# ScalarE copies the turned keys, squares the gated output and applies the first layer norm in place of VectorE

## What is computed

```python
q = rotate(silu(x @ Wq)); k = rotate(silu(x @ Wk)); v = x @ Wv      # per head
def step(S, qkv):                                                   # one chunk of 128 tokens
    scores = einsum('bthd,bshd->bhts', qi, ki) * D[None]            # D: causal mask with decay
    o_intra = einsum('bhts,bshd->bthd', scores, vi)
    o_inter = einsum('bthd,bhde->bthe', qi * decay_q, S)
    S_new = lam_C * S + einsum('bshd,bshe->bhde', ki * decay_k, vi)
    return S_new, o_intra + o_inter
g = o * sigmoid(x @ Wg1 @ Wg2)
g = g * rsqrt(mean(g * g, per head) + 1e-6) * norm_weight
x = layernorm(x + g @ Wo)
```

## Time and profile before

| | |
|---|---|
| time, three runs | 254.32, 258.5 and 258.65 us, median 258.5 |
| profiled execution, first to last instruction | 256.0 us |
| own time of the profiled execution | not listed; the three runs lie 1.7 below to 2.65 above its span |
| TensorE matmuls busy | 209.2 us (82%) |
| VectorE busy | 176.7 us (69%) |
| GpSimd busy | 114.0 us (45%) |
| ScalarE busy | 81.7 us (32%) |
| mean granted TensorE clock | 0.925 of full |

### The profile page before, as it was taken

One profiled execution on the slowest core, in us unless ns is written; L12 is line 12 of the kernel. 1 busy time (PEld: TensorE's weight loads), 2 busy tenths in 40 slices (PEclk: granted clock), 3 DMA queues, 4 the chain that ended last, 5 costly groups with the idle time before them and its releaser, 6 DMA issues.

```text
span 256.0 us, 3809 instructions
## 1 busy us (share of the span) xinstructions
PE 209.2 (82%) x1254; PEld 146.0 (57%) x1254; DVE 176.7 (69%) x438; ACT 81.7 (32%) x219; POOL 114.0 (45%) x188
## 2 busy tenths in 40 slices
PE   3788999995987798849799989999999997842461
PEld 1367555562745364515799776686786966411340
DVE  1168848779597979793556863348769788897751
ACT  0075664452432534241100113403223234423021
POOL 9661207335161413140516352346558529656352
PEclk9999999999799999977979999999999999995555
DMA  7990000000000000000000000000000001001011
GB/s 195 339 299 5 3 0 4 0 1 0 3 1 0 3 1 0 3 0 0 3 0 3 1 0 0 3 1 0 0 3 0 0 4 40 3 0 41 0 38 45
DMA packets 7027, 6.65 MB, mean 26 GB/s; under 512 B 1232, under 2 KB 6624, under 8 KB 7008
## 3 DMA queue, kind: packets, MB, share of 16 engines
q1 hardware_dynamic: 5744, 5.33, 6.6%
q10 hardware_dynamic: 1264, 1.08, 1.4%
HBM read 5.36 MB, written 1.05 MB: 25 GB/s over the span
## 4 chain that ended last, share of the span: by engine, by line
PE 52%; DVE 24%; issue 9%; POOL 6%; ACT 4%; DMA 3%; ACTq 1%; DVEq 0%; POOLq 0%
PE bank L1029 19%; PE bank L1230 12%; PE bank L1087 9%; PE bank L1244 4%; PE bank L1024 3%; DMA w_qk<-in_L_attn_Wk 3%; DVE hTe L776 2%; DVE w_qk L937 2%; PE bank L1132 2%; DVE stats L749 1%; POOL rstd L301 1%; DVE newton L685 1%; DVE probs L717 1%; PE bank L1120 1%; DVE newton L684 1%
## 5 line engine op out<-in xcount | busy, mean ns | idle before, releaser
L1087 PE MATMUL bank<-qx,kT 128*128 128x512 f32 x64 | 33.7, 652 | 10.6 <-DVE probs L717 8.9
L1230 PE MATMUL bank<-hTe,ctxT 128*128 128x128 f32 x256 | 31.7, 285 | 2.6 <-issue 2.6
L1230 PEld LDWEIGHTS bank<-hTe,ctxT 128*128 128x128 f32 x256 | 31.0, 201 | 3.2 <-issue 3.1
L499 ACT ACTIVATE qx<-bank,con 32x256 f32<-32x256 f32 x64 | 26.4, 458 | 16.0 <-PE bank L1024 15.4
L1244 PE MATMUL bank<-ctxT,aTe 128*128 128x256 f32 x128 | 29.0, 379 | 0.0
L284 POOL TENSOR_TENSOR rsin<-qk,rope_tab 128x256 f32<-128x256 f32 x16 | 13.2, 845 | 34.9 <-ACT qk L482 34.9
L1029 PE MATMUL bank<-f_w,oT 128*128 128x512 f32 (+4 forms) x80 | 28.0, 496 | 0.8 <-ACT oT L552 0.7
L298 POOL TENSOR_SCALAR rstd<-agg 128x1 f32<-128x1 f32 x24 | 5.3, 222 | 49.3 <-DVE agg L751 48.5
L1087 PEld LDWEIGHTS bank<-qx,kT 128*128 128x128 f32 x64 | 11.7, 197 | 26.8 <-issue 24.5
L717 DVE TENSOR_TENSOR probs<-bank,con 128x512 f32<-128x512 f32 x32 | 21.6, 686 | 5.8 <-PE bank L1087 5.0
L1244 PEld LDWEIGHTS bank<-ctxT,aTe 128*128 128x128 f32 x128 | 23.7, 190 | 2.9
(11 more groups left out here) (128 smaller groups left out, 407.7 us busy)
## 6 DMA issues: line engine op xcount, KB each, us to landing
x_sb<-in_x SPq DMA_DIRECT2D x4, 256.0 KB, 6.8
ctx_sb<-in_ctx SPq DMA_DIRECT2D x1, 1024.0 KB, 12.3
out<-x_sb SPq DMA_DIRECT2D x8, 128.0 KB, 1.7
fgo<-in_itok_BxS ACTq DMA_DIRECT2D x1, 512.0 KB, 9.3
con<-shape_constants SPq DMA_DIRECT2D x1, 338.5 KB, 3.0
w_v<-in_L_attn_Wv SPq DMA_DIRECT2D x1, 256.0 KB, 5.5
w_qk<-in_L_attn_Wq ACTq DMA_DIRECT2D x1, 256.0 KB, 5.7
w_qk<-in_L_attn_Wk ACTq DMA_DIRECT2D x1, 256.0 KB, 7.3
```

Source lines behind the costliest of these rows:

```text
L499: eng.activation(qx[rr, i % 2, :, 2 * r + par, :], two(bank[2][rr, 0:2 * P]), ACT.Copy, scale=con[rr, C_PARITY + par:C_PARITY + par + 1]). ...
L1087: eng.matmul(bank[3 + g % 2][:, :], kT[:, i % 2, g // 2, :], qx[:, i % 2, g // 2, 4 * (g % 2):4 * (g % 2) + 4, :].rearrange("p h n -> p (h ...
L1230: last = eng.matmul(bank[0][:, f * P:(f + 1) * P], ctxT[:, k, e, f * P:(f + 1) * P], hTe[:, j % 2, e, k, :], start=(e == 0 and k == 0), st ...
```

## The change

Three kinds of VectorE instructions go to ScalarE: the copy of the turned keys, the square of the gated output, and the application of the first layer norm. The last one has another form there (input times rstd plus a shift), so GpSimd computes that shift, minus mean times rstd, in one more instruction for each tile. Each engine's list is rewritten for it. On ScalarE the square stands ahead of the spreading of the queries and the key copy behind it. On VectorE the rest of `norm_o` moves behind `decay_state` (and, in round 7, behind the expert mask).

```diff
+            def ln0_scale(i):
+                ln_rstd(0, i)
+                eng.wait_ge(S_("ln0_rstd"), 2 * i + 2)
+                eng.tensor_scalar(shift[:, 0, i:i + 1], agg[:, 0, i, 0:1], rstd[:, 0, i:i + 1], -1.0,
+                                  ALU.mult, ALU.mult).then_inc(S_("ln0_shift"), 1)
...
-                        ln_rstd(0, i - 2)
+                        ln0_scale(i - 2)
...
+            def copy_kT(i):
+                eng.wait_ge(S_("kT_made"), i + 1)
+                if i >= 2:
+                    eng.wait_ge(S_("scores_made"), 4 * (i - 1))
+                eng.activation(kT[:, i % 2, :, :], two(bank[7][:, 0:D]), ACT.Copy).then_inc(S_("kT_copied"), 1)
+
+            def square_o(i):
+                eng.wait_ge(S_("gated"), i + 1)
+                if i >= 2:
+                    eng.wait_ge(S_("o_ms"), i - 1)
+                eng.activation(osq[:, i % 2, :], og[:, i % 2, :], ACT.Square).then_inc(S_("o_squared"), 1)
+
+            def apply_ln0(i):
+                eng.wait_ge(S_("ln0_shift"), i + 1)
+                eng.activation(h1[:, i, :], x1[:, i % 2, :], ACT.Identity, bias=shift[:, 0, i:i + 1],
+                               scale=rstd[:, 0, i:i + 1]).then_inc(S_("h1_done"), 1)
...
             def attention_round(i):
+                if i >= TILES:
+                    apply_ln0(i - 3)
+                if 0 <= i - 2 < TILES:
+                    square_o(i - 2)
                 if i < TILES:
                     expand_q(i)
+                    copy_kT(i)
                 if i + 1 < TILES:
                     silu_qk(i + 1)
+                if 0 <= i - 3 and i < TILES:
+                    apply_ln0(i - 3)
                 if i + 1 < TILES:
                     copy_v(i + 1)
...
             def attention_round(i):
-                if i < TILES:
-                    copy_kT(i)
...
-                if i >= TILES:
-                    ln_apply(0, i - 3, h1[:, i - 3, :], x1[:, (i - 3) % 2, :], "h1_done")
                 if 0 <= i - 2 < TILES:
                     gate_o(i - 2)
+                if i >= TILES and i - 2 < TILES:
                     norm_o(i - 2)
...
                 if i < TILES and i % 2 == 0:
                     decay_state(i // 2)
-                if 0 <= i - 3 and i < TILES:
-                    ln_apply(0, i - 3, h1[:, i - 3, :], x1[:, (i - 3) % 2, :], "h1_done")
+                if 0 <= i - 2 and i < TILES:
+                    norm_o(i - 2)
```

More of the change, by code:

```diff
@@ L151, in decoder_block @@
         rstd = sb("rstd", [P, 3, TILES])
-        shift = sb("shift", [P, TILES])
+        shift = sb("shift", [P, 2, TILES])
         newton = sb("newton", [P, 3, L * H])
@@ L425, in root_of_last @@
                             eng.wait_ge(S_("ln2_rstd"), 2 * n + 2)
-                            eng.tensor_scalar(shift[:, n:n + 1], agg[:, 2, n, 0:1], rstd[:, 2, n:n + 1], -1.0,
+                            eng.tensor_scalar(shift[:, 1, n:n + 1], agg[:, 2, n, 0:1], rstd[:, 2, n:n + 1], -1.0,
                                               ALU.mult, ALU.mult).then_inc(S_("shift"), 1)
@@ L464, in _ @@
                 if TILES <= r < TILES + 2:
-                    ln_rstd(0, r - 2)
+                    ln0_scale(r - 2)
         @block.scalar
@@ L582, in finish @@
                 eng.wait_ge(S_("shift"), j + 1)
-                eng.activation(y[:, ORDER[j], :], x3[:, j % 4, :], ACT.Identity, bias=shift[:, j:j + 1],
+                eng.activation(y[:, ORDER[j], :], x3[:, j % 4, :], ACT.Identity, bias=shift[:, 1, j:j + 1],
                                scale=rstd[:, 2, j:j + 1]).then_inc(S_("out_done"), 1)
@@ L705, in rope_add @@
                    .then_inc(S_("roped"), 1)
[L707 to L711, removed]
             def mask_scores(i, g):
@@ L736, in norm_o @@
             def norm_o(i):
-                eng.wait_ge(S_("gated"), i + 1)
-                eng.tensor_tensor(osq[:, i % 2, :], og[:, i % 2, :], og[:, i % 2, :], ALU.mult)\
-                   .then_inc(S_("o_squared"), 1)
                 eng.wait_ge(S_("o_squared"), i + 1)
```

## The result

The changed kernel takes 276.34 us in the median of four runs (273.76 to 278.52), the one before 256.42 beside it. The ratio is 1.077, with a 95% interval of 1.066 to 1.088: slower. The profiled execution took 276.38 us, 1.8 more than its span of 274.6, so 18.6 us were lost between first and last instruction (256.0 before). Each ratio of this document is taken against executions of the kernel before made beside the changed one; their medians were 256.2 to 257.7.

What follows compares the result with a forecast made beforehand. It asked which chain reaches score groups 2 and 3 last each round: VectorE's list, as before, or the new one over ScalarE. Round terms summed to +16.0 us; on the 258.5 median that gave 274.5, range 267 to 281.

Steps and rivals of the forecast that it cites:

- the first rival: ScalarE's gate, square, spreading, key copy chain decides the start of scores 2 and 3, rounds 2 to 7: loss 12 to 19 us; chance 0.74.
- the second one, the clock: Idle TensorE restarts slowly in three even rounds, 1.8 us each, 5.4 more in all: 280 us; chance 0.17.
- round 0: State matmuls wait for the key copy, ending at 28.0 where they had started at 26.87: +1.15 us.
- round 2: No residual; gate ends near 43.2, scores 2 and 3 start at 53.85 against 50.05: +3.8 us.
- round 3: Residual (T) to scores 2 and 3 (S) takes 8.2 against 8.7; 1.4 given back for the slow-clock tail: -1.9 us.
- round 5: From the residual's start (T) to scores 2 and 3 (S), 8.2 us against 7.95: +0.25 us.
- The square ahead of the spreading: ScalarE's square waits for the gate, so spreading ends at T + 5.3, was 3.6; later ScalarE work comes 1.7 us later.
- The key copy in even rounds: State matmuls wait 4 to 5 us for square, spreading and copy; +3.8, +4.1 and +4.15 us in rounds 2, 4, 6.
- The step that was mis-sized: Even rounds: slowed TensorE matmuls counted as hidden behind VectorE's decay and norm; scores 2 and 3 at T + 13.65 in round 6.
- Round 7: Expert mask waits for hT and stands ahead of the norm; score groups start at T + 11.95 against 7.9: +4.05 us.
- Rounds 8 to 10: ScalarE's norm application (0.60) replaces VectorE's (0.51) behind one more GpSimd instruction, mostly beside expert matmuls: +0.2 us.
- VectorE's relief: VectorE's list stays last, so each of rounds 2 to 7 saves 1.1 us: 252 us; chance 0.04.

Runs made afterwards that it cites:

- keys-first run: Changed kernel with the key copy moved to the front of ScalarE's round, ahead of square and spreading: 258.13 us, 1.007 of before.
- fill run: Changed kernel with two overwritten q and k projections in TensorE's idle time ahead of the state matmuls in rounds 2, 4 and 6: 274.39 us.
- with them mended: Changed kernel with the key copy first in ScalarE's round and the norm right behind the gate on VectorE: 251.29 us, 0.976 of before.
- the keys alone first: Kernel before with only the key copy on ScalarE, first in its round; square and layer norm on VectorE: 254.47 us, 0.997.
- the square back on VectorE: Changed kernel with the key copy first on ScalarE, the norm right behind the gate and the square on VectorE: 250.50 us, 0.974.
- the norm ahead: Changed kernel with the norm back right behind the gate on VectorE, ahead of the decay and round 7's expert mask: 268.48 us, 1.047.

## Why the prediction was right, and where not

The sign, the size and the main path held: forecast 274.5 with a range of 267 to 281, measured 276.34; in the profiles, +16.0 forecast and +18.6 measured. Part of the nearness of the totals is luck: the forecast started from 258.5, the median of three runs, and a fourth brought it to 256.42, so the loss between the medians is 19.9 us. That is over the 12 to 19 us of the first rival; the second one, the clock, came true in two of its three rounds. By its terms, from the rows above:

| term | forecast | measured |
|---|---|---|
| start of input | none | +0.3 |
| round 0 | +1.15 | +1.2 |
| round 1 | +0.2 | +0.4 |
| round 2 | +3.8 | +4.2 |
| round 3 | -1.9 | -2.5 |
| round 4 | +4.1 | +5.7 |
| round 5 | +0.25 | -0.3 |
| round 6 | +4.15 | +6.0 |
| round 7 | +4.05 | +4.6 |
| after | +0.2 | -1.0 |

- *The square ahead of the spreading.* Within 0.15 us of the forecast: the gate ends at T + 1.4 and the spreading at T + 5.15 in round 5 (93.05 + 3.36 with T at 91.26). The wrong part was the rotation behind it, put at 1.1 because of GpSimd beside it; it took 0.69 in rounds 3 to 6. The silu was 0.3 earlier too. The first mask ended at T + 7.5 and S came at T + 7.6, straight behind the first scores, which had waited for the spreading: both ways were about equally long. Hence -0.3 and not +0.25 in round 5, and S at 7.6 and not 8.2 in round 3.
- *The key copy in even rounds.* The state matmuls waited 5.34 and 4.88 us in rounds 4 and 6, within the 4 to 5 I named or just over, but 2.48 in round 2. That round still lost 4.2 us, since two Newton steps behind the copy took 0.74 and 0.65 in place of 0.17 to 0.18. The keys-first run shows that this place is what costs.
- *The step that was mis-sized* is "I have counted the slowed matmuls as hidden behind VectorE's decay and norm". S in round 6 was put at 13.65 and came at 15.5, in round 4 at 14.4 (10.3 and 4.1 more) and came at 16.1. The restart ran at half clock from the first matmul, so TensorE's branch, which I had ending 1.2 us ahead of the mask, became the later one; VectorE waited 0.75 us for its scores at 86.61. The clock rival's price of 1.8 per even round was near for rounds 4 and 6 (1.6 and 1.85 over the forecast), and wrong for round 2, where 2.48 us of idle time left the clock at 1.00. The fill run measures the clock's share in round 4 as 1.4.
- *Round 7.* S at 11.7 against 11.95, with errors that cancel: the expert mask took 0.69 and not 1.15, the norm 3.25 and not 2.65, since its first Newton step took 0.79 beside GpSimd's expert mask. The forecast equated its tail with before; it took 6.4 (133.77 to 140.21) and not 5.65, again at half clock.
- *Rounds 8 to 10.* They got 1.0 us shorter, since the stretch that before ran at 0.76 (7 us from 126.4 on) now ran at 1.00; see the last section.
- *VectorE's relief*, the third rival, is real, but in the changed kernel the orders hide it: with them mended the same work gives 0.976 in place of 1.077. The Trainium skill, "Perfetto Trace Analysis", section "Optimizing Scalar/DVE Operations", says that offloading from a saturated VectorE may make sense, and here it could pay. The Trainium skill, "ScalarE: Activation LUTs", section "Rules for kernel authors", would keep multiplications and additions on VectorE; the layer norm alone on ScalarE, dearer there (0.60 against 0.51), gave 0.978, so here the measurement is against it.

The single parts are each harmless or better (0.990, 0.984, 0.978), together they are 1.077. The reason is not load, for the same load in another order gives 0.976. It is that the key copy inherits the square's wait: copy behind spreading, spreading behind square, square behind the gate of another engine. The brackets of round 4 show this chain, and taking the copy out of it gives 18 us back. Not run were the square behind spreading and copy, and the square and the late copy without the layer norm, so how the square's wait and the spreading's length share the cost is read from traces alone.

## What to carry to other kernels

When an instruction moves to an idle engine, ask what it waits for and what stands behind it there: an engine that serves its list in order lends every later instruction the wait of an earlier one. Put what another engine is waiting for at the front of the list, and what waits for another engine at the back. Price an idle stretch on TensorE twice, for itself and for the clock of the restart, and check which of two parallel chains that end close together you are cutting.

## What the runs showed of the hardware

- The idle time ahead of a restart did not by itself decide the clock. After 2.04 us (round 5 before) and 2.48 us (round 2 after) the granted clock stayed at 1.00. After 2.83 us (round 3 before) the first scores still ran at full speed and the clock was 0.51 from 64 on, as in the earlier trace rows. After 5.34 and 4.88 us the very first matmuls ran at half. But with the keys alone first, rounds 3 and 4 of one execution stood the other way round, the shorter wait with the slow scores (0.50 from 63.4 on) and the longer one with the clock at 1.00:

```profile
62.37 2.71 PE L1094 MATMUL bank<-qx,kT 128*128 128x512 f32 x4 [2.29 <-DVE probs L725]
...
77.88 1.95 PE L1094 MATMUL bank<-qx,kT 128*128 128x512 f32 x4 [2.68 <-DVE probs L725]
```

  After 2.46 us, as good as the 2.48 above, round 4 of the kernel with the square back on VectorE went to the lower level too: its scores took 3.11 us. And with the norm ahead the clock was at half 2 us before the restart, in the changed kernel under 1 us before it, with the same idle time.
- The round behind round 7 (from its end to the next residual) took 18.6 us in seven of the thirteen kernels, with part of it at half clock, and 17.0 in the other six, at full clock, with nothing between. In all thirteen TensorE had stood idle for 1.97 to 1.99 us ahead of the experts' second tile. That stretch, before and after, with 5.0 us of matmul time in both but 30 matmuls in it at 0.76 and 43 at the full clock:

```profile
126.40:133.40 7.00, 5.03 (x30) 4.83 (x29) 5.35 (x16) 0.80 (x2) 2.72 (x3) 0.76 0.00 0
```

```profile
146.00:153.00 7.00, 5.01 (x43) 4.78 (x42) 4.15 (x16) 1.86 (x5) 2.76 (x4) 1.00 0.00 0
```

  A difference of a microsecond or two between two orders of this kernel can be the clock alone.
- Newton steps of VectorE that take 0.17 to 0.18 us took 0.74 and 0.65 while GpSimd's half of the rotation began beside them (52.69 and 53.47, GpSimd from 52.67, round 2 after). Where VectorE's rotation begins 0.14 us ahead of GpSimd's half, as in round 3 after, it takes 0.69, and 1.21 where GpSimd had begun 0.9 us before it. In round 5 before it took 1.10 with GpSimd's half just over (86.37 to 87.81, the rotation from 88.09) and only its scaling of the output beside it, begun 0.17 us earlier; in round 2 after, where the rotation began 0.16 us ahead of that scaling, it took 0.68.
